# A four-layer attention kernel: who makes and carries the banded attention's strips, and the loop order of the second feed-forward layer

## The reference

```python
mask = (j <= i) & (i - j < W)                       # W = 64
bias = slopes[:, None, None] * (j - i).astype(x.dtype)[None]
sa = _mha(x, x, swq, sbq, swk, sbk, swv, sbv, swo, sbo, mask, bias)
x = _layernorm(x + sa, g1, be1)
ca = _mha(x, mem, cwq, cbq, cwk, cbk, cwv, cbv, cwo, cbo, None, None)
x = _layernorm(x + ca, g2, be2)
ff = jax.nn.gelu(x @ w1 + b1, approximate=False) @ w2 + b2
return _layernorm(x + ff, g3, be3)
```

## Time and profile before

| | |
|---|---|
| Time, median of 3 runs | 1622.87 us (1618.45 to 1623.59) |
| The profiled execution | 1621.18 us, its span 1619.4 us |
| PE busy | 1430.6 us, 88% of the span |
| DVE busy | 875.5 us, 54% |
| ACT busy | 721.2 us, 45% |
| POOL busy | 262.8 us, 16% |
| Mean granted TensorE clock | 0.955 |

### The profile page before, as it was taken

The page is one execution under the profiler, slowest core; times in us unless marked ns, Lnnn a source line. Parts: engine busy times, 40 slices in busy tenths (PEclk is TensorE's granted clock), DMA queues, the critical chain, the costliest instruction groups (busy, mean ns, idle before and its releaser), DMA issues.

```text
span 1619.4 us, 24001 instructions
## 1 busy us (share of the span) xinstructions
PE 1430.6 (88%) x8176; PEld 714.0 (44%) x8204; DVE 875.5 (54%) x2135; ACT 721.2 (45%) x1185; POOL 262.8 (16%) x129
## 2 busy tenths in 40 slices
PE   5999798888999888888899988888899998989886
PEld 2336455423533654532443554553253355455334
DVE  2662664584266356567355446546636635655761
ACT  0662253355266234427446425352725632725461
POOL 1004131301100412210110213221011040313001
PEclk9999899989999989998999988988999998999899
DMA  9001304303200220530310022242031004033210
GB/s 354 1 1 28 84 2 92 69 11 111 67 1 7 39 66 1 101 69 1 124 54 1 8 53 53 46 78 48 3 122 53 1 7 104 2 72 60 39 59 13
DMA packets 44775, 85.28 MB, mean 53 GB/s; under 512 B 10464, under 2 KB 27872, under 8 KB 44384
## 3 DMA queue, kind: packets, MB, share of 16 engines
q1 hardware_dynamic: 40112, 71.07, 17.3%
q10 hardware_dynamic: 4528, 12.49, 3.7%
HBM read 43.68 MB, written 2.10 MB: 28 GB/s over the span
## 4 chain that ended last, share of the span: by engine, by line
PE 61%; DVE 18%; issue 11%; ACT 5%; DMA 3%; ACTq 2%; POOL 0%; DVEq 0%; POOLq 0%
PE ring L1264 7%; PE obank L1274 7%; PE ring L1220 7%; DVE nmax L1061 7%; PE ring L1429 6%; PE ring L1254 6%; PE ring L1241 3%; PE ring L1330 3%; PE obank L1479 3%; PE ring L1178 3%; PE ring L1420 3%; ACTq L689 2%; DMA q_all<-q_parts 2%; ACT q_all L758 2%; PE ring L1207 2%
## 5 line engine op out<-in xcount | busy, mean ns | idle before, releaser
L1061 DVE TENSOR_REDUCE nmax<-ring 128x2 f32<-128x1024 f32 (+1 forms) x192 | 218.6, 1175 | 54.1 <-PE ring L1429 36.4
L659 ACT ACTIVATE region_e<-region_d,nmin 128x512 f32<-128x512 f32 x256 | 182.7, 714 | 81.7 <-DVE nmin L914 80.0
L914 DVE CUSTOM_DVE_ANT_0 region_d<-ring,maskb 128x512 f32<-128x512 f32 x256 | 165.9, 686 | 92.7 <-issue 92.5
L771 ACT ACTIVATE region_e<-ring 128x1024 f32<-128x1024 f32 x192 | 183.4, 991 | 58.3 <-PE ring L1429 35.0
L758 ACT ACTIVATE q_all<-ring 2x1024 fp32r<-2x1024 bf16 x96 | 97.5, 1015 | 204.8 <-PE ring L1490 204.3
L585 POOL TENSOR_TENSOR nat_x<-nat_n,rows 128x1024 f32<-128x1024 f32 x16 | 37.6, 2351 | 640.3 <-DVE nat_n L959 472.8
L1420 PE MATMUL ring<-cbf 64*128 64x128 bf16 (+2 forms) x1280 | 133.6, 289 | 0.0
L1264 PE MATMUL ring<-region_q 64*128 64x512 f32 x512 | 126.9, 615 | 6.8 <-ACT region_q L648 5.4
L1057 DVE TENSOR_REDUCE nmax<-ring 128x4 f32<-128x512 f32 (+1 forms) x96 | 86.1, 911 | 79.5 <-PE ring L1420 78.7
L1274 PE MATMUL obank<-region_e,vs 128*64 128x512 f32 x512 | 124.0, 605 | 0.0
L1429 PE MATMUL ring<-k_tiles_a,q_all 64*128 64x512 f32 (+4 forms) x384 | 79.2, 454 | 24.2 <-DMA q_all<-q_parts 15.5
(11 more groups left out here) (178 smaller groups left out, 2205.5 us busy)
## 6 DMA issues: line engine op xcount, KB each, us to landing
q_all<-q_parts SPq DMA_DIRECT2D x160, 64.0 KB, 2.8
q_all<-q_parts ACTq DMA_DIRECT2D x128, 64.0 KB, 3.4
region_e<-in_w_f SPq DMA_DIRECT2D x8, 1024.0 KB, 6.0
k_tiles_a<-k_parts SPq DMA_DIRECT2D x96, 64.0 KB, 2.3
k_tiles_b<-k_parts SPq DMA_DIRECT2D x96, 64.0 KB, 2.3
wvo<-in_wv SPq DMA_DIRECT2D x5, 1024.0 KB, 5.3
wqk<-in_wq SPq DMA_DIRECT2D x4, 1024.0 KB, 9.6
wqk<-in_wk SPq DMA_DIRECT2D x4, 1024.0 KB, 11.5
```

The lines of the kernel that those rows point to most:

```text
L659: ins = act.activation(e0[:, n % E0, h, :], sm0[:, n % 2, h, :], ACT.Exp, bias=nmin0[:, n, h:h + 1], scale=-1.0, accum_out=sum0[:, n, h:h ...
L771: act.activation(e16[:, n % 4, 2 * u:2 * u + 2, 0:nq], slot((a, "B", g, kt, u))[:, :, 0:nq], ACT.Exp)\
L914: ins = dve.tensor_tensor_reduce(out=sm0[:, n % 2, h, :], in0=slot(("S0", p, kt))[:, h, :], in1=maskb[:, :], scale=-1.0, scalar=3.0e38, op ...
L1061: dve.tensor_reduce(nmax[:, qt, 2 * u:2 * u + 2], slot(name)[:, :, 0:nk], AX.X, ALU.max, negate=True)\
```

## The change

Four edits. The banded keys' weights `w_sk` are multiplied by 1/4 once, by POOL before the loop, so that the projection comes out scaled. ACT then makes only the high keys, and DVE makes the low keys straight from PSUM, with the bias, as it does for queries; the slot `KS` is given back by DVE, and POOL's split for the banded attention is gone. The low query strips of groups 0 and 1 are issued by SP instead of ACT, in the causal and the banded attention; in the banded one SP issues them between the key strips, and its first key strips wait for the high keys alone. The second feed-forward layer loops over contraction tiles outside and over the four row tiles inside, and waits for each pair of hidden tiles on its own.

```diff
@@ def stack(a, b), the sync queue @@
-                sp.wait_ge(*drained_by(K_JOB[a], b))
+                sp.wait_ge(*((k_hi_ready, (b + 1) * DT) if a == BANDED else drained_by(K_JOB[a], b)))
...
-                if a != BANDED:
-
-                    sp.wait_ge(k_split, b * 3 + a + 1)
-                    for g in range(GROUPS):
+                if a == BANDED:
+
+                    stack_k(a, b, 0, k_high)
+                    sp.wait_ge(*drained_by(K_JOB[a], b))
+                    stack_k(a, b, 0, k_low)
+                    sp.wait_ge(*drained_by(Q_JOB[a], b))
+                    stack_q(a, b, 0, q_strips[2:])
+                    stack_k(a, b, 1, k_high + k_low)
+                    stack_q(a, b, 1, q_strips[2:])
+                    for g in (2, 3):
                         stack_k(a, b, g, k_high + k_low)
-                else:
-
-                    stack_k(a, b, 0, k_high)
-                    sp.wait_ge(k_split, b * 3 + a + 1)
-                    stack_k(a, b, 0, k_low)
-                    for g in (1, 2):
-                        stack_k(a, b, g, k_high + k_low)
+                        stack_q(a, b, g, q_strips)
+                    return
+                sp.wait_ge(k_split, b * 2 + 1)
+                for g in range(GROUPS):
+                    stack_k(a, b, g, k_high + k_low)
                 sp.wait_ge(*drained_by(Q_JOB[a], b))
-                stack_q(a, b, 2, q_strips)
-                if a == BANDED:
-                    stack_k(a, b, 3, k_high + k_low)
-                stack_q(a, b, 3, q_strips)
+                for g in (0, 1):
+                    stack_q(a, b, g, q_strips[2:])
+                for g in (2, 3):
+                    stack_q(a, b, g, q_strips)
@@ POOL, once before the loop @@
+            pool.wait_ge(k_loaded["ls"], 64)
+            pool.tensor_scalar(w_sq["sk"][:, :, :], w_sq["sk"][:, :, :], DH ** -0.5, None, ALU.mult).then_inc(keys_scaled, 1)
@@ POOL, in the loop @@
-                split_k(BANDED)
@@ def stack_q(a), the scalar queue @@
-                    for at in (0, 1):
-                        strip(0, at, 0)
-                    if a == FULL:
+                    for g in (0, 1):
                         for at in (0, 1):
-                            strip(1, at, 0)
-                        return
-                    act.wait_ge(*drained_by(Q_JOB[a], b))
-                    strip(0, 3, 1)
-                    for at, part in ((0, 0), (1, 0), (3, 1)):
-                        strip(1, at, part)
+                            strip(g, at, 0)
@@ ACT @@
-                drain_k(("KS",), BANDED, 1, ACT.Identity)
+                act.wait_ge(*filled_by(("KS",), b))
+                for t in range(DT):
+                    act.activation(k_parts_of[BANDED][:, 0, t, :], slot(("KS",))[:, t, :], ACT.Identity, bias=kcol[:, 1, t:t + 1]).then_inc(k_hi_ready, 1)
@@ DVE, ahead of drain_q(1, ...) @@
+                for t in range(DT):
+                    dve.wait_ge(k_hi_ready, b * DT + t + 1)
+                    ins = dve.scalar_tensor_tensor(out=k_parts_of[BANDED][:, 1, t, :], in0=slot(("KS",))[:, t, :], scalar=kcol[:, 1, t:t + 1],
+                                                   in1=k_parts_of[BANDED][:, 0, t, :], op0=ALU.add, op1=ALU.subtract)
+                ins.then_inc(*ends_drain(("KS",)))
@@ PE @@
+                pe.wait_ge(keys_scaled, 1)
                 project_x(2, ("KS",), w_sq["sk"], range(DT))
...
-                for j in range(FT // 2):
-                    pe.wait_ge(*drained_by(("F1", j), b))
-                out_project("F2", w_f2, hid, FT)
+                dst = [start(("F2", j)) for j in range(2)]
+                for t in range(FT):
+                    if t % 2 == 0:
+                        pe.wait_ge(*drained_by(("F1", t // 2), b))
+                    for j in range(2):
+                        for i in range(2):
+                            m = 2 * j + i
+                            ins = pe.matmul(dst[j][:, i, 0:D], hid[:, t, m * P:(m + 1) * P], w_f2[:, t, :], start=(t == 0), stop=(t == FT - 1))
+                        if t == FT - 1:
+                            ins.then_inc(*ends_fill(("F2", j)))
```

12 lines of the change are left out of this document (3 added, 9 removed).

## The result

The changed kernel takes 1611.5 us (median of 4 runs, 1608.7 to 1613.6), the kernel before beside it 1621.6 (1618.5 to 1623.6): ratio 0.9937, 95% interval 0.9920 to 0.9953, so 10 us faster. The prediction said 1610, with 1604 to 1617.5 as its range; it was counted from a median of 1622.9 for the kernel before. The profiled execution is the slowest of the four, 1613.6 us with a span of 1611.8.

What follows compares the result with a forecast made beforehand. PE bounds most of the span, with waits on DVE and ACT. Second layer 5.4, banded start 4.4 and clock 3 sum to 12.8 us, taking the median 1622.9 to 1610; range 1604 to 1617.5.

Steps and rivals of the forecast that it cites:

- Second layer: Second feed-forward layer: PE's 1.36 us wait for the last GELU goes in four elements, 5.4 us, up to 0.8 more.
- rival "slower": Second layer: rotating through four PSUM areas costs over 0.05 us a record; 1636 at 0.1 us. Chance 0.06.
- Keys' low parts: Banded keys: DVE makes low parts from PSUM; SP starts 1.2 us earlier, but by itself the path gains nothing.
- Banded start: Banded attention's start: group 1's query strips land earlier, PE then waits 0.91 us for DVE; 4.4 us over four elements.
- The transfer rival: Banded start: strips bound by transfer, not issue, so group 1's queries land as late; 1617.5. Chance 0.12.
- Clock: After the banded start: shorter waits bring back full clock in elements that fell; 3 us taken, bounds 5.4 gained, 1.8 lost.
- the clock gives nothing or takes a little: After the banded start: no clock gain, cuts of 9.8 us, or 8 if element 1 falls; 1613 to 1615. Chance 0.22.
- ACT's wait for group 3's keys: Banded attention: later key strips still land before ACT's exponential of group 0's last key tile; cover 1 us, cost 0.
- Causal: Causal attention: the same strips move to SP, but PE waits 1.65 us for DVE's maxima, so 0.

Runs made afterwards that it cites:

- the repeat: The changed kernel run once more, unchanged: 1611.4 us (6 runs), ratio 0.9938 to the kernel before.
- half the bytes: The changed kernel with group 1's banded strips carrying half their bytes, the rest left stale: 1611.8 us, ratio 0.9948 to the kernel before.
- none, three and eight: Filler matmuls ahead of group 1's banded scores: changed kernel without them 1614.9 us, with its own three 1611.5, with eight 1613.8.
- strips only: The kernel before with only the new order of strips on both queues: 1616.3 us, ratio 0.9975.
- keys only: The kernel before with scaled weights, DVE's low keys and SP's early start, low query strips left with ACT: 1626.6 us, ratio 1.0040.
- the second profile with eight fillers: The changed kernel with eight instead of three filler matmuls ahead of group 1's banded scores, run again: 1613.3 us, ratio 0.9945.

## Why the prediction held, step by step

- **Second layer, 5.4 (up to 0.8 more).** Right in mechanism, with the size at the upper end: 6.07 ahead of the layer, 1.52 an element. Each is the wait of 1.36 and 0.16 of the 0.2 that an idle gap leaves out. The stretch from there on is another 0.9 to 1.1 shorter: 0.4 of it is the run itself (13.98 us and not 14.08), and the rest is hardly more than scatter, for kernels with the old loop order read 78.8 to 79.6 there and those with the new one 78.4 to 78.9. Four PSUM areas in turn cost nothing: 63 steps in 13.6 us, 0.22 each, so the rival "slower" falls.
- **Keys' low parts, nothing by themselves.** Wrong as a statement on this part alone: alone it costs 6.5 us. The step that failed is "by itself this part gives SP 1.2 us and the path nothing". In the whole change the early start is worth 1.6, through the strips.
- **Banded start, 4.4.** 3.7 measured (column A, 79.10 to 75.38; 3.9 in the repeat). The failed step is "with ACT's queue done by then they land in some 2.6 us". ACT's queue is done issuing, at 649.7, but not done moving: its eight strips take 4.2 us at the median from issue to landing. The last of group 1 goes out 0.7 us later than forecast, takes 3.6, and lands 15.0 us after the first high keys (655.53, less 640.50), where 13.4 was forecast (659.3 less 645.88). The term came out nearly whole because PE would have waited for DVE anyway: of the late strips only about 0.4 us an element is paid (18.81 against 18.41).
- **The transfer rival (0.12)** had the cause and a wrong result. The Trainium skill's rule (DMA: Bandwidth & Descriptors, Issuing engines are not separate DMA queues) is borne out in that the transfers share their engines and that issuing group 1's low queries on the other queue saved no landing (16.0 us after the first high keys and not 15.0). The order still counts: which strips travel first was worth 2.3 us, and letting strips that nobody awaits travel among them costs 4.8 (A, 75.38 to 80.20) to 6.6 (79.10 to 85.68).
- **Clock, 3.** Column B fell by 0.5 and half clock by 6.8 us: a sixth of the term. The failed step is that the three elements with the longer waits for strips would come back once the strips are on time: with the strips on time (half the bytes) the clock fell in three elements as before. So the waits for strips alone do not decide it; how much fell went with the fillers, 37.5, 17 and 0 to 6.8 us for none, three and eight, and eight brought no gain in time. Elsewhere the clock took back at least as much (layer 0, above). So the rival "the clock gives nothing or takes a little", 9.8 us and 1613, names what happened: the gain was 10.1 and not 12.8. That 1611.5 lies as near to 1610 as to 1613 is in part luck, since the kernel before measured 1621.6 beside it and not 1622.9. The Trainium skill's statement (TensorE: Matmul & The Clock Gate, Part 1) that the monitor behind the clock is not reset by a kernel agrees with the two profiles of one kernel, whose stretches at half clock lie in different elements.
- **ACT's wait for group 3's keys, 0 by a cover of 1 us.** The cover held where the clock fell for 6.8 us and failed in elements 0 and 1, where it fell for 3.4 and not at all: 1.17 and 1.30 us of waiting. C shows 1.5 lost, 0.9 in the repeat. The last key strip lands at 667.2, 26.7 us after the first high keys; 24.5 was forecast (670.4 less 645.88). The forecast had no term for what came: 0.7 us by the slow issues beside ACT's queue, and 1.5 us by the instruction packet. Without the packet both strips would have landed 0.2 to 0.3 us before ACT was ready, an estimate (the landing less the 1.5 us above 2.3, and 0.2 from a landing to ACT's start); of the nine waits in other profiles eight would keep 0.4 to 1.0 us, so the packet is not the whole cause there.
- **Causal, 0**: from its queries' projection to the banded keys' the traces read 294.6 before, 295.5 after and 295.3 in the repeat, 295.1 and 295.0 with this part unchanged. No gain, and a loss of half a microsecond could not be told from scatter. **The slower case**: nothing in the traces for it.

The sum of what the profile shows in the changed stretches is 6.1 + 1.1 + 2.7 = 9.9, and the medians show 10.1. This is closer than it deserves: the two spans differ by 7.6 (8.9 with the repeat), since the clock took 5.5 (2.0) in layer 0 and gave 3.1 (1.2) in the cross attention.

What stays open: why the same 16 engines move 162 and not 194 GB/s. In the slow windows both queues move strips of one group (its keys from `k_parts`, its queries from `q_parts`, the same partitions), in the fast ones of different groups; with strips only the rate was 177 to 186, with keys only 173 to 184. No run tried a pairing by itself, so that is a suspicion. Open too is what share of the late landings of group 1 is the instruction packet's.

## What to carry to other kernels

Where two queues feed the same engines, ask what is in flight, not only what is issued: put what is awaited first on both, and let nothing that isn't awaited start early, for it stalls the issues and delays the landings of the rest. Look at what a wait hides before pricing its end; here DVE's maxima were ready only 0.4 us ahead of what the late strips allowed. And do not book a gain of clock from one profile: the fillers put half clock from 37 us to nothing at this place, and none of the 3 to 5 us expected from it reached the median.

## What the runs showed of the hardware

- A 64 KB strip lands 2.3 us after its issue when one queue works, and 2.8 to 5.5 us when two do in the changed kernel; single issues then take 1.3 to 1.9 us and not 0.6 (2.03 us for two of them at 650.63).
- A 16 KB packet of the queue `instruction` among strips of 64 KB goes with a landing after 2.9 to 3.8 us instead of 2.3 (eleven cases), though the 16 engines were far from full (share 0.4 between 664 and 667 us, as q1's 37.5% and q8's 3.1% show).
- The engines' busy share was 1.0 at 162 and at 194 GB/s alike. The share alone does not say what is being moved.
- Half clock stood for 3.4, 6.8 or 10.2 us at a time at the banded starts (once 13.7, keys only), with no level between the two. It fell also where PE had waited no longer than 1.6 us at a time: in element 1 of the second profile with eight fillers its waits are 0.19 and 1.57, and the clock reads 0.95.
